# Where TensorE makes the outer products of a spline convolution that runs beside an attention: six of 32 tiles moved ahead

## The chip, the core and the metric

The kernel runs on one core of a Trainium2 chip. It is one launch. Its metric is the device time in microseconds, from start to end, of that core; a run's time is one execution, and three runs are given for the kernel before. The engines are TensorE (PE; its weight loads are PEld), VectorE (DVE), ScalarE (ACT), GpSimd (POOL) and SyncE (SP). Each runs its own stream of instructions, and they wait for one another by semaphores.

## What is computed

The reference is a graph network of four layers on 3125 nodes with 32 features and 103,125 edges: an attention, a mean aggregation in two steps, a mixture of Gaussians, and a spline convolution. The part that matters here is one stage in which two things are computed edge by edge, both sorted by target node.

```python
# attention (layer 0), per head; src is the target of the sum
e = leaky_relu(a_src[:, src] + a_dst[:, dst] + fc_b)
e = exp(e - seg_max(e, src)[:, src])
out = segment_sum(e * hp[:, dst, :], src) / segment_sum(e, src)
# second spline convolution (inside layer 3): 64 -> 64 features, K = 125 = 5**3 kernel points
basis, idx = spline_basis(pseudo)          # 8 of 125 weights per edge
msg[e] = sum_s basis[e, s] * (h[col[e]] @ W[idx[e, s]])
out = segment_sum(msg, row) / deg + b
```

The kernel writes the eight weights of an edge as a row of 125 (mostly zero). Then the sum over edges of (basis row) x (feature row) is a 125 x 64 matrix, an outer product per chunk of edges, and the weights W are applied to it afterwards.

## The kernel before, in words

The stages run one after the other. The change touches only `stage_attention_spline` (L840), which runs once, and in it only the stream of TensorE, with the helper `outer_products` of the class `Spline` (L1380), which other stages call too, without the new argument.

**Tiling.** The sorted edges lie in chunks of 16 slots of one target node. A tile is 128 slots, that is 8 chunks; a block is 32 tiles (TB), so 256 chunk columns; there are 37 blocks, two in each turn of a hardware loop, the last one behind it.

**One block n, engine by engine.**

- POOL gathers the table rows of the far ends (`gather`, L940 to L951): 32 indirect DMAs, one a tile, into one of two buffers. It may start when the sums (`summed`) and the spreads (`sl.spreads`) of the block that last used the buffer are made.
- ScalarE copies out the attention term (L1122), takes the exponentials (L1126), copies the weighted sums out of PSUM (L1135, two copies, semaphore `copied`), takes two small exponentials (L1140), copies the turned rows of block n-1 (L1114) and then the outer products, two copies for each pair of tiles, 32 in all (L1460, `outers`), and the turned spline rows (L1466).
- VectorE makes the scores (L1065 on), the basis rows in two halves (L1330), two of the eight spreads of features over chunks (`sl.spread(..., lead)`, L1351, four tiles each), then the probabilities spread over chunks (L1079, `spreads`), the running sums of block n-1 (L1036, L1361), the factors, and the six other spreads. A spread from the third on waits until the products of the four tiles that used its buffer are made.
- SP loads records, near ends and factors.
- TensorE (`one`, L981): turns the term (L989); applies the spline weights to the outer products of block n-1 (`through_weights`, L1418, 64 matmuls in the program); turns the exponentials (L994); makes the 32 weighted sums (L999); turns the rows of block n-1 (`turn_rows`, L977, and `sl.turn`, L1431); makes the outer products of block n (L1405), two a tile, 64 in all. A float32 matmul shows as two in the trace, except where its moving side is turned against the identity.

**What sets the order** is the code: each engine's stream is written out by hand, and nothing reorders it.

**PSUM.** The outer products go round three pairs of banks, two tiles a pair (0 and 1, 2 and 3, 4 and 5). Banks 4 and 5 also hold the weighted sums. So the tiles 4 and 5 wait until ScalarE has copied the sums (`third=(copied, n + 2)`), and from tile 6 on each pair waits for the copies (`outers`) of the pair before it in the same banks. The weighted sums of block n+1 need no such wait on the outer products, since `through_weights` has waited for them all.

**Names in the profile.** at_bank is any PSUM bank; at_spread and at_far are the spread probabilities and the gathered rows; p_spread, p_basis and p_outer belong to the spline.

Of the kernel before, what the change touches and what calls it, by code (L numbers as in the profile page):

```python
# [31 lines left out]
TB = 32  # L32
# [807 lines left out]
def stage_attention_spline(nc, g, weights, sums64):  # L840

    o = g.R
    C8, S, V = o.per_tile, o.chunk, o.vb
    W, parts = 4 * (F + 1), V // P
    with ExitStack() as c:
# [38 lines left out]
        turned, shifts, probs, turned_back, spreads, summed, copied = (  # L886
            sem(n) for n in ("turned", "shifts", "probs", "turned_back", "spreads", "summed", "copied"))
        rec_v = o.rec.rearrange("(p t) w -> p t w", p=P)
        sl = Spline(nc, c, g, "p_2", 64, 64, sums64, shared=(rec, far, F + 5, far_in, 16 * TB))
# [5 lines left out]
        with nc.Block() as block:  # L895
# [66 lines left out]
            def _(pe):  # L962
# [18 lines left out]
                def one(n, b, first=False):  # L981

                    pe.wait_ge(terms, n + 1)
                    pe.wait_ge(shifts, n + 1)
                    if not first:

                        pe.wait_ge(spreads, n)
                        pe.wait_ge(rows_copied, n)
                    nc.tensor.transpose(turned_square, term[:].rearrange("p t h -> p (t h)"), g.ident[:]).then_inc(turned, 1)  # L989
                    if not first:  # L990
                        sl.through_weights(pe, n - 1)

                    pe.wait_ge(probs, n + 2)
                    nc.tensor.transpose(turned_square, prob[:], g.ident[:]).then_inc(turned_back, 1)  # L994

                    pe.wait_ge(spreads, n + 1)
                    pe.wait_ge(copied, n + 1)
                    for t in range(TB):
                        last = nc.tensor.matmul(ps_sum[t // (TB // 2)][:, t % (TB // 2), :, :], far[b][:, t, 0:F + 1],  # L999
                                                spread[:, t, :, :], start=True, stop=True)  # L1000
                    last.then_inc(summed, 1)
                    if not first:
                        turn_rows(n - 1, 1 - b)
                        sl.turn(pe, n - 1)

                    sl.outer_products(pe, n, third=(copied, n + 2))

                one(0, 0, first=True)
                one(1, 1)
# [172 lines left out]
class Spline:  # L1182
# [194 lines left out]
        self.nc.tensor.matmul(self.ps_shift[:].rearrange("p t d -> p (t d)"), self.o.mask_t[:],  # L1377
                              self.shift[b][:].rearrange("c t d -> c (t d)"), start=True, stop=True).then_inc(self.shifts, 1)

    def outer_products(self, pe, m, third=None):  # L1380
        ring = len(self.ps_outer)
        for t in range(TB):
            if t % self.HT == 0:

                pe.wait_ge(self.bases, m * 2 + (t // self.HT + 1))
# [1092 lines left out]
```

## Time and profile before

| | us |
|---|---|
| median of 3 runs | 8911.31 |
| lowest and highest | 8875.33 and 8933.79 |
| the profiled execution | 8838.25 |
| its span | 8835.3 |

| engine | busy us | share |
|---|---|---|
| TensorE, matmuls | 5190.5 | 59% |
| TensorE, weight loads | 3677.3 | 42% |
| POOL | 4537.0 | 51% |
| VectorE | 4063.1 | 46% |
| ScalarE | 1650.5 | 19% |

The shares are of the whole program. The stage of the change takes 2,345 to 4,725 us of the span, some 27% of it, and has to be read by itself. In rows in order of time, the first number is the start, the second the length of a merged run of instructions, and the bracket the engine's idle time before it with what ended it; "issue" is time in which the engine waited for nothing that the profile shows, "remote" a release that it can't name.

### The profile page before, as it was taken

How to read it: one execution, taken by the hardware profiler on the slowest of the kernel's cores; microseconds unless marked ns; L12 is line 12 of the kernel's file. 1: busy time of each engine (PE TensorE's matmuls, PEld its weight loads, DVE VectorE, ACT ScalarE, POOL GpSimd, SP SyncE). 2: the span in 40 equal slices, each digit the busy share in tenths (PEclk: the TensorE clock that was granted, in tenths of full speed). 3: DMA queues.
4: the chain of work that ended last, by engine and by line, in shares of the span. 5: the costliest groups of instructions: out<-in, count | busy, mean ns of one | idle time of the engine just before them, and what ended most of it. 6: DMA issues, size and time to landing. Idle time of an engine off the chain costs nothing. (4 is left out here: it accounts for less than half of the span.)

```text
span 8835.3 us, 94325 instructions
## 1 busy us (share of the span) xinstructions
PE 5190.5 (59%) x31067; PEld 3677.3 (42%) x31067; DVE 4063.1 (46%) x8022; ACT 1650.5 (19%) x2811; POOL 4537.0 (51%) x4319
## 2 busy tenths in 40 slices
PE   4333333866366666666664546898887346445544
PEld 4333333645355555555543323444444224333333
DVE  6454444779444444444442213565555234433343
ACT  1111110148323232322321000000000112111111
POOL 3666664010355545555552243565553676777664
PEclk9999998679777777777776768899898667667676
DMA  3222210023311111111684533111111111111175
GB/s 67 65 65 61 63 60 19 21 91 157 87 38 37 37 36 37 36 38 37 35 36 111 203 110 139 29 30 29 28 29 26 18 15 17 17 15 18 15 14 14
DMA packets 388446, 441.45 MB, mean 50 GB/s; under 512 B 241139, under 2 KB 312320, under 8 KB 387981
## 3 DMA queue, kind: packets, MB, share of 16 engines
q0 software_dynamic: 137696, 130.26, 14.4%
q1 hardware_dynamic: 191113, 286.63, 10.1%
q10 hardware_dynamic: 59568, 23.69, 1.2%
q8 instruction: 38, 0.62, 0.0%
q14 instruction: 31, 0.25, 0.0%
HBM read 358.46 MB, written 82.34 MB: 50 GB/s over the span
## 5 line engine op out<-in xcount | busy, mean ns | idle before, releaser
L950 POOL DMA_INDIRECT at_far<-att_table,at_rec x1184 | 1268.2, 1071 | 1476.0 <-DVE p_spread L1351 714.8
L1507 POOL DMA_INDIRECT p_far<-table,p_rec x1184 | 1322.0, 1117 | 652.9 <-issue 357.8
L2137 PE MATMUL g_l_ps_sum<-g_l_row,g_l_of 128*128 128x400 f32 x3224 | 1192.3, 526 | 195.4 <-issue 170.2
L2067 POOL DMA_INDIRECT g_l_got<-table,g_l_index x806 | 805.7, 1000 | 551.6 <-DVE g_l_index L2075 308.3
L1405 PE MATMUL p_ps_outer<-p_spread,p_basis 128*25 128x40 f32 (+1 forms) x4736 | 834.5, 355 | 384.0 <-issue 236.3
L533 POOL DMA_INDIRECT rec_r<-so_r_rec,so_r_place x806 | 814.0, 1010 | 455.4 <-issue 232.1
L2137 PEld LDWEIGHTS g_l_ps_sum<-g_l_row,g_l_of 128*128 128x128 f32 x3224 | 638.9, 199 | 749.3 <-issue 301.8
L1405 PEld LDWEIGHTS p_ps_outer<-p_spread,p_basis 128*25 128x25 f32 (+1 forms) x4736 | 669.9, 190 | 554.1 <-issue 377.7
L488 PE MATMUL so_r_look<-so_r_table,so_r_lo_t 128*128 128x26 f32 x1612 | 425.1, 434 | 787.5 <-DVE so_r_table L432 745.9
L2079 DVE TENSOR_SCALAR g_l_row<-g_l_iota,edge_row 128x800 f32<-128x800 f32 x806 | 485.3, 676 | 575.3 <-remote 417.5
L488 PEld LDWEIGHTS so_r_look<-so_r_table,so_r_lo_t 128*128 128x128 f32 x1612 | 417.5, 356 | 796.8 <-DVE so_r_table L432 570.9
L1418 PE MATMUL at_bank<-p_outer,p_w 125*64 125x256 f32 x4736 | 647.7, 422 | 56.7 <-issue 51.2
L1405 PE MATMUL at_bank<-p_spread,p_basis 64*125 64x256 f32 x4736 | 655.1, 432 | 23.1 <-ACT p_outer L1460 12.3
L1351 DVE TENSOR_TENSOR p_spread<-p_far,mask_r 128x1024 f32<-128x1024 f32 x296 | 359.1, 1224 | 639.5 <-PE p_ps_outer L1405 318.1
L1460 ACT COPY p_outer<-at_bank 125x512 f32<-125x512 f32 x1184 | 589.7, 727 | 108.0 <-PE at_bank L1405 98.2
L1405 PEld LDWEIGHTS at_bank<-p_spread,p_basis 64*125 64x125 f32 x4736 | 540.3, 210 | 129.0 <-ACT p_outer L1460 33.3
L1418 PE MATMUL p_ps_out<-p_outer,p_w 125*32 125x256 f32 (+1 forms) x2738 | 375.7, 440 | 307.1 <-issue 235.2
L1418 PEld LDWEIGHTS at_bank<-p_outer,p_w 125*64 125x64 f32 x4736 | 438.8, 152 | 254.7 <-issue 167.7
L999 PE MATMUL at_bank<-at_spread,at_far 128*33 128x32 f32 x2368 | 200.4, 227 | 550.0 <-issue 489.6
L1460 ACT COPY p_outer<-p_ps_outer 125x512 f32<-125x512 f32 x592 | 345.6, 586 | 810.8 <-PE p_ps_outer L1405 389.7
L1351 DVE TENSOR_TENSOR p_spread<-at_far,p_mask 128x1024 f32<-128x1024 f32 x296 | 359.1, 1223 | 258.1 <-PE at_bank L1405 245.9
L999 PEld LDWEIGHTS at_bank<-at_spread,at_far 128*33 128x33 f32 x2368 | 153.8, 141 | 598.9 <-issue 535.6
(456 smaller groups left out, 5907.8 us busy)
## 6 DMA issues: line engine op xcount, KB each, us to landing
adjacent<-ad_by_chunk SPq DMA_DIRECT2D x74, 800.0 KB, 3.3
so_r_row<-pad_src SPq DMA_DIRECT2D x62, 832.0 KB
g_l_counts<-adjacent SPq DMA_DIRECT2D x60, 800.0 KB
g_l1d_counts<-adjacent SPq DMA_DIRECT2D x59, 800.0 KB
so_r_low<-pad_lo_src SPq DMA_DIRECT2D x62, 416.0 KB
at_far<-att_table,at_rec POOLq DMA_INDIRECT x1184
p_far<-table,p_rec POOLq DMA_INDIRECT x1184
rec_r<-so_r_rec,so_r_place POOLq DMA_INDIRECT x806
```

What stands on the lines that cost most here:

```text
L488: last = nc.tensor.matmul(ps_look[b][:, j, :], lo_t[b][:, :, j], table[b][:, :, j], start=True, stop=True)
L533: pool.indirect_dma_start(out=o.rec[:, :], out_offset=bass.IndirectOffsetOnAxis(ap=place[b][:, j:j + 1], axis=0), in_=rec[b][:, j, :], in_ ...
L950: pool.indirect_dma_start(out=far[b][:, t, :], out_offset=None, in_=g.att_table[:, :], in_offset=bass.IndirectOffsetOnAxis(ap=rec[b][:, t, ...
L999: last = nc.tensor.matmul(ps_sum[t // (TB // 2)][:, t % (TB // 2), :, :], far[b][:, t, 0:F + 1], spread[:, t, :, :], start=True, stop=True)
L1351: nc.vector.tensor_mul(self.spread_to[s % 2][:], rows.unsqueeze(3).to_broadcast(bx), self.mask[:].unsqueeze(1).unsqueeze(1).to_broadcast(b ...
L1405: last = self.nc.tensor.matmul(to.rearrange("k f c -> k (f c)"), basis[part, t % self.HT, :], rows[part, t % self.XT, :, :].rearrange("p f ...
L1418: last = self.nc.tensor.matmul(to, self.w[:, f, :], self.outer[:, f, :], start=(f < self.G), stop=(f >= self.J - self.G))
L1460: self.nc.scalar.copy(to[:, :, :, r, :], self.ps_outer[q % len(self.ps_outer)][r][:]).then_inc(self.outers, 1)
L1507: pool.indirect_dma_start(out=sl.far[b][:, t, :], out_offset=None, in_=table[:, :], in_offset=bass.IndirectOffsetOnAxis(ap=sl.rec[b][:, t, ...
L2067: pool.indirect_dma_start(out=got[b][:, j, :], out_offset=None, in_=table[:, :], in_offset=bass.IndirectOffsetOnAxis(ap=index[b][:, j:j + ...
L2079: last = nc.vector.tensor_scalar(row1[b][:, j, :], iota[:], g.edge_row[:, bass.ds(step * HB + j, 1)], None, ALU.is_equal)
L2137: last = nc.tensor.matmul(ps_sum[k][:], of4[b][:, j, :, :].rearrange("p k f -> p (k f)"), row1[b][:, j, k * COLS:(k + 1) * COLS], start=Fa ...
```

## The change

TensorE's order within a block is another one. The first four tiles' outer products are made after the turned exponentials and ahead of the weighted sums, tiles 4 and 5 between the sums and the turning of rows, and the other 26 after the turning. `outer_products` takes the range of tiles; its waits are the same, each in front of the same tile. The first block of all has no turning. All stages that call `outer_products` without a range are as before. The other engines' instructions and their order are unchanged.

```diff
@@ stage_attention_spline, tensor, one(n, b)
                     pe.wait_ge(probs, n + 2)
                     nc.tensor.transpose(turned_square, prob[:], g.ident[:]).then_inc(turned_back, 1)
 
+
+                    sl.outer_products(pe, n, tiles=range(0, 2 * sl.BT))
+
                     pe.wait_ge(spreads, n + 1)
                     pe.wait_ge(copied, n + 1)
                     for t in range(TB):
                         last = nc.tensor.matmul(ps_sum[t // (TB // 2)][:, t % (TB // 2), :, :], far[b][:, t, 0:F + 1],
                                                 spread[:, t, :, :], start=True, stop=True)
                     last.then_inc(summed, 1)
+
+                    sl.outer_products(pe, n, third=(copied, n + 2), tiles=range(2 * sl.BT, 3 * sl.BT))
                     if not first:
                         turn_rows(n - 1, 1 - b)
                         sl.turn(pe, n - 1)
-
-                    sl.outer_products(pe, n, third=(copied, n + 2))
+                    sl.outer_products(pe, n, tiles=range(3 * sl.BT, TB))
 
@@ class Spline
-    def outer_products(self, pe, m, third=None):
+    def outer_products(self, pe, m, third=None, tiles=range(TB)):
         ring = len(self.ps_outer)
-        for t in range(TB):
+        for t in tiles:
```

Here `sl.BT` is 2. In the program's order on TensorE, one block of the loop reads so before, from the turned exponentials (L994) to the first products that wait for the sums' copy:

```order
L994 MATMUL at_bank<-ident,at_prob 128x128 [waits at_probs]
L999 MATMUL at_bank<-at_spread,at_far 33x32 [waits at_copied,at_spreads]
L999 MATMUL at_bank<-at_spread,at_far 33x32 x31
L977 MATMUL at_bank<-ident,at_run 128x33 [waits at_scanned,at_rows_copied]
L977 MATMUL at_bank<-ident,at_run 128x33 x7
L1431 MATMUL at_bank<-p_fold,p_run 128x64 [waits p_2_scanned,p_2_copied]
L1431 MATMUL at_bank<-p_fold,p_run 128x64
L1385 ISA
L1388 ISA [waits p_2_bases]
L1405 MATMUL at_bank<-p_spread,p_basis 125x256 [waits p_2_spreads]
L1405 MATMUL at_bank<-p_spread,p_basis 125x256 x7
```

and so with the change (its lines are numbered up to 5 higher: L995 is L994 before, L1003 is L999, L1410 is L1405):

```order
L995 MATMUL at_bank<-ident,at_prob 128x128 [waits at_probs]
L1390 ISA
L1393 ISA [waits p_2_bases]
L1410 MATMUL at_bank<-p_spread,p_basis 125x256 [waits p_2_spreads]
L1410 MATMUL at_bank<-p_spread,p_basis 125x256 x7
L1003 MATMUL at_bank<-at_spread,at_far 33x32 [waits at_copied,at_spreads]
L1003 MATMUL at_bank<-at_spread,at_far 33x32 x31
L1393 REGISTER_ALU
L1410 MATMUL at_bank<-p_spread,p_basis 125x256 [waits at_copied,p_2_spreads]
L1410 MATMUL at_bank<-p_spread,p_basis 125x256 x3
```

Eight matmuls, tiles 0 to 3 (16 in the trace), now stand ahead of the 32 sums, with the waits for the bases and the first spread; the four of tiles 4 and 5, with the wait for the sums' copy, follow the sums directly.

The second place is the turning of rows and what follows it. Before, the products of tiles 4 and 5 led straight on to tile 6 with its wait for the product copies:

```order
L1388 REGISTER_ALU
L1405 MATMUL at_bank<-p_spread,p_basis 125x256 [waits at_copied,p_2_spreads]
L1405 MATMUL at_bank<-p_spread,p_basis 125x256 x3
L1403 ISA
L1405 MATMUL at_bank<-p_spread,p_basis 125x256 [waits p_2_outers]
L1403 REGISTER_ALU
L1405 MATMUL at_bank<-p_spread,p_basis 125x256 [waits p_2_outers]
```

With the change the turning (L978 and L1436, before L977 and L1431) comes between them:

```order
L978 MATMUL at_bank<-ident,at_run 128x33 [waits at_scanned,at_rows_copied]
L978 MATMUL at_bank<-ident,at_run 128x33 x7
L1436 MATMUL at_bank<-p_fold,p_run 128x64 [waits p_2_scanned,p_2_copied]
L1436 MATMUL at_bank<-p_fold,p_run 128x64
L1408 ISA
L1410 MATMUL at_bank<-p_spread,p_basis 125x256 [waits p_2_outers]
L1408 REGISTER_ALU
L1410 MATMUL at_bank<-p_spread,p_basis 125x256 [waits p_2_outers]
```

The turning is now queued behind the wait for the sums' copy, and tile 6 behind the turning.

## Rows read from the trace of the kernel before

A, B and C are three blocks of the stage: A turns its term at 3566.65 us, B at 2991.65, C at 2412.59.

**Rows 1.** groups by line, attention stage: count, busy us, mean ns, idle before.
```profile
L950 POOL DMA_INDIRECT at_far<-att_table,at_rec x1152 | 1238.0, 1075 | 1055.2 <-DVE p_spread L1351 714.8 <-issue 340.4
...
L999 PE MATMUL at_bank<-at_spread,at_far 128*33 128x32 f32 x2368 | 200.4, 227 | 550.0 <-issue 489.6 <-DVE at_spread L1079 59.3
```

**Rows 2.** waits of the same stretch: who, for whom, us in total, times, longest.
```profile
POOL at_far L950 <- DVE p_spread L1351: 714.8, 35, 22.5
```

**Rows 3.** order of time, POOL, block A: start us, us, what, idle before.
```profile
3561.31 0.94 POOL L950 DMA_INDIRECT at_far<-att_table,at_rec  x1 [17.54 <-DVE p_spread L1351]
...
3603.87 0.94 POOL L950 DMA_INDIRECT at_far<-att_table,at_rec  x1 [0.30 <-issue]
3624.97 0.94 POOL L950 DMA_INDIRECT at_far<-att_table,at_rec  x1 [20.16 <-DVE p_spread L1351]
```

**Rows 4.** order of time, TensorE, block A.
```profile
3576.16 9.40 PE L1418 MATMUL at_bank<-p_outer,p_w 125*64 125x256 f32 x80 [0.28 <-issue]
3585.48 0.33 PE L994 MATMUL at_bank<-ident,at_prob 128*128 128x128 f32 x1
3587.81 1.39 PE L999 MATMUL at_bank<-at_spread,at_far 128*33 128x32 f32 x37 [2.00 <-DVE at_spread L1079]
...
3607.70 0.33 PE L999 MATMUL at_bank<-at_spread,at_far 128*33 128x32 f32 x3 [1.14 <-issue]
3607.95 1.06 PE L977 MATMUL at_bank<-ident,at_run 33*128 33x33 f32 x8
3608.94 1.11 PE L1431 MATMUL at_bank<-p_fold,p_run 128*128 128x64 f32 x4
3609.99 16.86 PE L1405 MATMUL at_bank<-p_spread,p_basis 64*125 64x256 f32 x128
```

**Rows 5.** order of time, TensorE, block B.
```profile
3012.06 1.90 PE L999 MATMUL at_bank<-at_spread,at_far 128*33 128x32 f32 x43 [1.60 <-issue]
...
3017.35 0.29 PE L999 MATMUL at_bank<-at_spread,at_far 128*33 128x32 f32 x2 [0.29 <-issue]
```

**Rows 6.** order of time, ScalarE, block B.
```profile
3032.98 1.06 ACT L1135 COPY at_sums<-at_bank 33x512 f32<-33x512 f32 x2 [39.16 <-remote]
```

**Rows 7.** order of time, POOL, block B.
```profile
3029.38 0.94 POOL L950 DMA_INDIRECT at_far<-att_table,at_rec  x1 [0.30 <-issue]
3048.72 0.94 POOL L950 DMA_INDIRECT at_far<-att_table,at_rec  x1 [18.40 <-DVE p_spread L1351]
```

**Rows 8.** order of time, ScalarE, block A.
```profile
3608.06 1.06 ACT L1135 COPY at_sums<-at_bank 33x512 f32<-33x512 f32 x2 [39.29 <-PE at_bank L999]
...
3609.64 0.35 ACT L1114 COPY at_rows<-at_bank 128x264 f32<-128x264 f32 x1
...
3612.11 1.07 ACT L1460 COPY p_outer<-at_bank 125x512 f32<-125x512 f32 x2 [2.11 <-PE at_bank L1405]
3613.81 14.79 ACT L1460 COPY p_outer<-at_bank 125x512 f32<-125x512 f32 x30 [0.63 <-PE at_bank L1405]
```

**Rows 9.** order of time, VectorE, block A.
```profile
3586.53 1.22 DVE L1079 TENSOR_TENSOR at_spread<-at_bank,mask_r 128x1024 f32<-128x1024 f32 x1 [6.74 <-PE at_bank L994]
...
3622.96 1.23 DVE L1351 TENSOR_TENSOR p_spread<-at_far,p_mask 128x1024 f32<-128x1024 f32 x1 [0.73 <-PE at_bank L1405]
```

**Rows 10.** windows in block A: length, busy us, granted clock, DMA share, GB/s.
```profile
3572.80:3589.80 17.00, 14.16 (x144) 11.22 (x141) 10.10 (x9) 0.00 (x0) 13.56 (x11) 1.00 0.17 34
3589.80:3613.70 23.90, 10.42 (x55) 7.32 (x56) 5.24 (x12) 3.01 (x7) 11.46 (x12) 0.50 0.17 37
3613.70:3630.80 17.10, 13.20 (x115) 11.12 (x111) 7.35 (x6) 15.28 (x32) 4.61 (x5) 1.00 0.12 29
```

**Rows 11.** order of time, TensorE, block C.
```profile
2431.58 2.40 PE L999 MATMUL at_bank<-at_spread,at_far 128*33 128x32 f32 x59 [1.32 <-issue]
...
2457.07 15.26 PE L1405 MATMUL at_bank<-p_spread,p_basis 64*125 64x256 f32 x104 [11.55 <-ACT p_outer L1460]
```

**Rows 12.** order of time, POOL, block C.
```profile
2470.52 0.94 POOL L950 DMA_INDIRECT at_far<-att_table,at_rec  x1 [16.95 <-DVE p_spread L1351]
```

## The prediction

> **What bounds the kernel now.** I read the page first, then, for the attention stage alone (2,345 to 4,725 us, 37 blocks of about 64 us), the groups by line, then each engine's order of time in one block, then three blocks that go otherwise, then the clock by windows. The groups show who repeats without slack: POOL's gathers are 1152 times 1075 ns with 340 us of short gaps between them, and 714.8 us in which POOL waits for VectorE's last spread [rows 1], in 35 waits [rows 2], so 20.4 us each. 1238.0 + 340.4 + 714.8 = 2293 us of a stage of 2377. A block is therefore 43.5 us of gathers (3561.31 to 3604.81) and then some 20 us until the next gathers may start (3624.97) [rows 3]. The change can only shorten or lengthen those 20 us.
>
> What lies in them, in the block that I call A: TensorE's outer products, weighted sums and so on go on during the gathers, but not at their own pace. The 64 weighted-sum matmuls start at 3587.81; 37 are through in 1.39 us, and the other 27 take until 3608.04, with gaps of multiples of 0.7 us that the profile puts down to "issue" [rows 4], 489.6 us in the stage [rows 1]. They end 3.2 us after the last gather of the block has been issued. That this is no coincidence shows in block B: its sums are through at 3017.64 [rows 5], yet ScalarE's copy of them, which waits for nothing else that is late, starts only at 3032.98 [rows 6], 2.7 us after the last gather ended at 3030.32 [rows 7]. Towards the end of the gathers every engine's stream is held up, and it comes free about 2.7 us after them. I call this moment the release: about 3607.5 in A.
>
> After it, in A: sums copied by ScalarE 3608.06 to 3609.12, rows turned 3607.95 to 3609.01, spline rows turned to 3610.05, outer products from 3609.99 [rows 4, 8]. ScalarE's copies of the products are back to back from 3613.81, 30 in 14.79 us, 0.493 each, 0.99 for the two of a bank pair (two tiles) [rows 8]. VectorE's last spread, which needs 24 tiles of products, starts at 3622.96 [rows 9], and the gathers 2 us later [rows 3]. So from the release on the chain is: sums, turning, ScalarE's first product copy, then ScalarE's pace. TensorE's own pace is near it: 0.1175 us a matmul at full clock (80 in 9.40 [rows 4]), 0.94 for two tiles; but at half clock, until 3613.70 [rows 10], double that, 1.88.
>
> **The change part by part.** It moves instructions on TensorE only and adds no copy, transfer or semaphore. Each of the 37 blocks keeps 128 outer-product matmuls.
>
> *Four tiles ahead of the sums.* 16 matmuls (4 tiles, two halves, two passes) at 0.1175 are 1.88 us, at full clock since the window before 3589.80 has 1.00 [rows 10]. TensorE now waits 2.33 us there (3585.48 to 3587.81) for VectorE's turning of the probabilities [rows 4, 9]. Both spreads that they need are made earlier, and the banks are free. So they are hidden: 0 us. If that cover is gone (the spread came at once), they cost 1.88 us at that place, but the sums' end is set by the release.
>
> *The sums themselves.* What counts is how many of them are done at the release. If TensorE gets through a fixed number of instructions before it, 16 more stand in front and 16 sums are left over; at the pace of the 37, 0.038 us, they cost 16 x 0.038 = 0.6 us. If instead the stream goes on being filled while TensorE is busy and stops filling while it stands, all are done early, and ScalarE's copy starts 2.7 instead of 3.25 us after the last gather [rows 3, 6, 7, 8]: -0.6 us. Nothing in this trace has TensorE busy at just that place. The waits there differ from block to block, and after a short one the sums run further before they trickle: 59 after 1.32 us idle in block C [rows 11], 43 after 1.60 in B [rows 5], 37 after 2.00 in A [rows 4]; that speaks for the second. I take -0.1 us and keep -0.6 and +0.6.
>
> *Two tiles between sums and turning.* This is where the change adds a wait. The third bank pair is the one that holds the sums, so TensorE stands until both sum copies are through: 3609.12, where before it turned rows from 3607.95 on. Then 8 matmuls at half clock, 1.88 us, to 3611.1. The turning is queued behind: 1.06 us for the attention rows gives 3612.15, and ScalarE, which waits for them in front of its product copies, copies the rows at about 3612.4 instead of 3609.64, 2.7 us later [rows 4, 8]. It needs its 0.35 us and a DMA command, 0.6 us as before (3609.64 to about 3610.6). Its first product copy starts at about 3613.35 against 3612.11, with three bank pairs ready. Before, the second pair began at 3613.81, delayed by TensorE at half clock; now it begins at 3613.35 + 0.99 = 3614.34. **The product copies run 0.5 us later** from there on.
>
> *26 tiles after the turning.* Tile 6 needs the first copies of the first pair (two take 1.07 us together [rows 8], so 0.6 for one and up to 1.1 for both; I take 0.75), so about 3614.1, and 1.88 us at half clock ends at 3616.0; ScalarE wants it at 3613.35 + 3 x 0.99 = 3616.3. It holds. For the next pair ScalarE would wait 0.6 us if the clock is still at half. So what was won in front (1.88 us of work at full clock that was 3.76 at half) is used up: it had been TensorE's time, and the end was ScalarE's. I take +0.55 for the whole chain after the sums, bounds -0.1 (TensorE's own chain: turned at 3613.2, 72 matmuls, 8 of them at half clock, 1.88 + 64 x 0.1175 = 9.4, 3622.6 against 3622.7) and +1.1 (0.5 + 0.6).
>
> *VectorE* has its third spread free earlier, since four tiles are done; its later ones follow the pace above. Its spread of the probabilities, row updates and the DMA queues of SP and ScalarE keep their order; the two row stores go out some 2.7 us later and are needed a block later. The copy of the term, weights and the next turning (ScalarE's tail) move by the same 0.5 us, beside the gathers: 0.
>
> *Three blocks of 37 like B* lose what they had. There TensorE turned rows and made products before the release, and the wait for VectorE was 18.40 us [rows 7] instead of 20.4. Now the turning stands behind a copy that ScalarE makes only at the release: 3 x 2.0 = 6 us.
>
> Sum: 36 x (-0.1 + 0.55) + 6 = 22 us. The profiled execution took 8838.25 us (span 8835.3), so 8860 in its terms; it lies 73 us under the median of the three runs, 8911.3 (8875.3 to 8933.8), on which I put the forecast: **8933 us**. About 1% (89 us) is what a measurement of this kernel can tell from no change.
>
> **The rivals.**
> 1. *The sums finish early and ScalarE does not fall behind*: -0.6 and -0.1 a block, 36 x -0.7 = -25, less 6 lost: 8892 us. For: the blocks with short waits. Against: the copy of rows is moved behind 8 matmuls and 1.1 us of waiting. 0.18.
> 2. *A fixed number of instructions before the release and the full delay after it*: +0.6 + 1.1 = 1.7, x 36 + 6 = +67: 8978 us. For: the 27 sums that trickle at 0.7 us. Against: the trickle comes after standing still. 0.16.
> 3. *Clearly faster*: block C. Its ScalarE got its copies through in the midst of the gathers; TensorE stood 11.55 us for the next product copy [rows 11], and POOL waited 16.95 us [rows 12]. If filling TensorE's wait made every block so: 36 x (16.95 - 20.4) = -124: 8787 us, 1.4% faster. Against: C was the second block, and in B ScalarE got nothing though the sums were done. 0.04.
> 4. *Clearly slower, by the clock.* It is half from 3589.80 to 3613.70 and full then, 5.7 us after TensorE became busy without a pause [rows 4, 10]. The change puts two pauses there (1.1 us for the sums' copy, about 0.9 us for tile 6). If these keep the clock at half until the end of the products, the nine pairs from tile 6 to tile 23 take 1.88 us: 3614.1 + 16.9 = 3631.0, and the last spread comes 8 us later: 36 x 8 = +288: 9199 us, 3.2% slower. It decides from the point where the clock is not full by about 3616.3, where ScalarE wants tile 6's pair; each further pair at half costs 0.9 us. Against: in the window up to 3589.80 TensorE stands 2 us before the sums, and the clock is full throughout [rows 4, 10]; it falls in the trickle, not in that pause. 0.06.
>
> The Trainium skill (TensorE: Matmul & The Clock Gate, HAM oscillation — how this bites in real kernels) speaks for rival 4: waits between groups of matmuls let the clock fall, and every group starts slow. By that rule, the trace agrees that the clock falls while the sums trickle; whether pauses of 1 us keep it low, no row here shows.
>
> **How the numbers follow.** The forecast has 0.52, rivals 1 to 4 have 0.18, 0.16, 0.04 and 0.06, and 0.04 is left for a mere shift of all runs. The runs scatter by some 30 us around their median. From rival 1 less 30 to rival 2 and some 25: 8862 to 9003, which leaves out rivals 3 and 4 and some of the shift. Faster by over 1%: rival 3, 0.04. Slower by over 1%: rival 4 and a little of rival 2, 0.08. The rest, 0.88, is within.
>
> **What would show it.** 16 outer products between the turned probabilities and the sums, starting within 0.2 us of the former. TensorE idle about 1.1 us before the 8, released by ScalarE. The rows' copy about 4.3 us after the sums end (1.6 before). POOL's wait for the last spread: 20.4 us before, 20.9 expected; under 19.9 speaks for rival 1, over 21.7 for rival 2, under 18 for rival 3, over 25 for rival 4, with a granted clock at half beyond the first pair after the turning. I would be wrong altogether if ScalarE's copy of the sums began well before the last gather's end, or if the 43.5 us of gathers themselves changed.

## The result, and the profile after

| | us |
|---|---|
| the kernel before, median of 10 runs | 8885.85 (8856.58 to 8933.79) |
| the changed kernel, median of 10 runs | 8990.35 (8959.49 to 9037.11) |
| ratio, 95% interval | 1.012 (1.0097 to 1.0144) |
| profiled execution of the changed kernel | 8987.28, span 8985.1 |

The change costs 1.2%, 104 us, where 22 us were forecast and "within 1%" had 0.88. Compared twice more, on two chips, it gave 1.0113 (1.0086 to 1.014) and 1.011 (1.0078 to 1.0142), so the sign is not in doubt. 8990.35 lies within 8862 to 9003, but the change is nearly five times as large as forecast; the kernel before, measured beside it, had 8885.85, some 25 us under the median on which the forecast was put.

The groups by line of the stage, and its waits, in the changed kernel (they answer to [rows 1, 2]):

```profile
L951 POOL DMA_INDIRECT at_far<-att_table,at_rec x1168 | 1240.2, 1062 | 1215.3 <-DVE p_spread L1356 870.0 <-issue 345.3
...
L1003 PE MATMUL at_bank<-at_spread,at_far 128*33 128x32 f32 x2368 | 159.8, 238 | 605.6 <-issue 388.8 <-DVE at_spread L1084 216.6
```
```profile
POOL at_far L951 <- DVE p_spread L1356: 870.0, 35, 28.0
```

The gathers are what they were: 1062 ns each against 1075, and short gaps of 0.3 us. POOL's wait for the last spread grew from 714.8 to 870.0 us, by 155.2; the span grew by 149.8 (8985.1 - 8835.3). The loss is in the 35 waits: 24.9 us each instead of 20.4. One block of the changed kernel on TensorE and ScalarE, in order of time (the places of [rows 4, 8]):

```profile
3660.72 3.57 PE L1003 MATMUL at_bank<-at_spread,at_far 128*33 128x32 f32 x64 [17.89 <-DVE at_spread L1084]
3665.84 1.13 PE L1410 MATMUL at_bank<-p_spread,p_basis 64*125 64x256 f32 x8 [1.55 <-ACT at_sums L1140]
3666.78 0.67 PE L978 MATMUL at_bank<-ident,at_run 33*128 33x33 f32 x8
3667.38 1.11 PE L1436 MATMUL at_bank<-p_fold,p_run 128*128 128x64 f32 x4
3669.95 14.37 PE L1410 MATMUL at_bank<-p_spread,p_basis 64*125 64x256 f32 x104 [1.46 <-ACT p_outer L1465]
```
```profile
3664.64 1.06 ACT L1140 COPY at_sums<-at_bank 33x512 f32<-33x512 f32 x2 [43.63 <-DVEq L1045]
...
3668.29 0.35 ACT L1119 COPY at_rows<-at_bank 128x264 f32<-128x264 f32 x1
...
3669.31 3.03 ACT L1465 COPY p_outer<-at_bank 125x512 f32<-125x512 f32 x6 [0.67 <-ACT at_rows L1119]
3672.54 1.07 ACT L1465 COPY p_outer<-at_bank 125x512 f32<-125x512 f32 x2 [0.20 <-PE at_bank L1410]
3674.23 11.85 ACT L1465 COPY p_outer<-at_bank 125x512 f32<-125x512 f32 x24 [0.62 <-PE at_bank L1410]
```

Two waits stand where the diff put them: 1.55 us for the sums' copy ahead of the 8 matmuls of tiles 4 and 5, and 1.46 us for the first product copy ahead of tile 6. ScalarE copies three ready bank pairs back to back and then waits for TensorE twice, 0.20 and 0.62 us. This block shows one thing more: TensorE stood 17.89 us for VectorE's spread probabilities. In this execution they came over 5 us after the turned exponentials (called late from here on) in 30 of 33 blocks; in two later profiles of the same kernel in 5 of 33, with ratios nearly as high. So the terms are read from the last pair of profiles below.

### The profile page after: what moved, and what is told of

Same layout as the page of the kernel before. It is cut to its first block and busy times, and to the rows that moved or that the text cites. A ratio compares the mean times of both kernels' runs of the same rounds, so it can differ in the third digit from the quotient of the medians.

```text
span 8985.1 us, 94325 instructions
## 1 busy us (share of the span) xinstructions
PE 5210.8 (58%) x31067; PEld 3736.3 (42%) x31067; DVE 4064.9 (45%) x8022; ACT 1660.2 (18%) x2811; POOL 4548.7 (51%) x4319
## 5 line engine op out<-in xcount | busy, mean ns | idle before, releaser
L1410 PE MATMUL p_ps_outer<-p_spread,p_basis 128*25 128x40 f32 (+1 forms) x4736 | 825.7, 353 | 354.4 <-issue 204.1
L1410 PEld LDWEIGHTS p_ps_outer<-p_spread,p_basis 128*25 128x25 f32 (+1 forms) x4736 | 665.1, 188 | 520.5 <-issue 354.6
L1410 PE MATMUL at_bank<-p_spread,p_basis 64*125 64x256 f32 x4736 | 695.0, 443 | 99.8 <-ACT at_sums L1140 48.2
L1423 PE MATMUL at_bank<-p_outer,p_w 125*64 125x256 f32 x4736 | 678.6, 438 | 72.1 <-issue 67.7
L1410 PEld LDWEIGHTS at_bank<-p_spread,p_basis 64*125 64x125 f32 x4736 | 586.6, 216 | 166.5 <-issue 72.1
L1423 PEld LDWEIGHTS at_bank<-p_outer,p_w 125*64 125x64 f32 x4736 | 466.1, 158 | 274.0 <-issue 184.4
L1003 PE MATMUL at_bank<-at_spread,at_far 128*33 128x32 f32 x2368 | 159.8, 238 | 605.6 <-issue 388.8
L1003 PEld LDWEIGHTS at_bank<-at_spread,at_far 128*33 128x33 f32 x2368 | 142.7, 156 | 636.4 <-issue 410.8
```

Source lines behind the costliest of these rows:

```text
L1410: last = self.nc.tensor.matmul(to.rearrange("k f c -> k (f c)"), basis[part, t % self.HT, :], rows[part, t % self.XT, :, :].rearrange("p f ...
L1423: last = self.nc.tensor.matmul(to, self.w[:, f, :], self.outer[:, f, :], start=(f < self.G), stop=(f >= self.J - self.G))
```

## The experiments

All ratios are to the kernel before on the same chip, with 95% intervals. Means over blocks are over the 33 blocks of the loop whose gathers wait (the two first left out), worked out from the rows of each trace. "Copy" is the start of ScalarE's copy of the sums after the end of the block's last gather, in us; "the hold-up" is what the prediction describes, the slow trickle of the other engines' streams towards the end of the gathers, and "the release" its end.

**Which half of the change costs?** `e1` keeps the four tiles ahead and puts the turning right behind the sums; `e2` has nothing ahead and makes tiles 0 to 5 between sums and turning; `e3` is the changed kernel with TensorE's wait for the spread probabilities in front of the four tiles; `e4` is e1 with that wait. As edits of the changed kernel:

```diff
 e1, e4, behind the sums:
-  sl.outer_products(pe, n, third=(copied, n + 2), tiles=range(2 * sl.BT, 3 * sl.BT))
   if not first: turn_rows(n - 1, 1 - b); sl.turn(pe, n - 1)
-  sl.outer_products(pe, n, tiles=range(3 * sl.BT, TB))
+  sl.outer_products(pe, n, third=(copied, n + 2), tiles=range(2 * sl.BT, TB))
 e2:
-  sl.outer_products(pe, n, tiles=range(0, 2 * sl.BT))
-  sl.outer_products(pe, n, third=(copied, n + 2), tiles=range(2 * sl.BT, 3 * sl.BT))
+  sl.outer_products(pe, n, third=(copied, n + 2), tiles=range(0, 3 * sl.BT))
 e3, e4, ahead of the sums:
-  sl.outer_products(pe, n, tiles=range(0, 2 * sl.BT))
   pe.wait_ge(spreads, n + 1)
+  sl.outer_products(pe, n, tiles=range(0, 2 * sl.BT))
```

(These pieces of code, and those below, are cut to the lines that matter.)

> Four tiles' outer products stay ahead of the weighted sums, the other 28 go back behind the turning of rows, so that no wait stands between the sums and the turning. Theory W (waking): when TensorE goes straight on after the turned exponentials, VectorE's spread of them (median 2.1 us after in the kernel before, 14.9 in the changed one) comes late, and with it the sums. Then this kernel keeps that: median about 15 us, sums ending about 3 us later than before; but the product copies start sooner after the sums, so POOL's wait is about 22 us (20.4 before, 24.9 changed) and the time about 1.006 of before. Rival T (turning): the loss comes from the wait between sums and turning. Then this kernel is at or under before (ratio 0.995 to 1.000). Rival N (number): only the number of TensorE instructions ahead of the sums' end counts; like W here in the sums (16 more ahead).

> Nothing ahead of the sums; the tiles 0 to 5 all stand between the sums and the turning. Theory W: VectorE's spread comes 2 us after the turned exponentials as before and the sums end as before; the turning is queued behind 24 matmuls at half clock and the sums' copy (about 5.6 us), so the first product copy comes some 3.8 us later than before, of which 0.7 is won back: POOL's wait about 23.5 us, ratio about 1.012, by another way than in the changed kernel. Rival T: the same, and it would be the whole of the changed kernel's loss. What tells them apart is the median from turned exponentials to VectorE's spread: 2 (W), and whether the loss per tile of delay is as large as that of the changed kernel.

> The changed kernel with one edit: TensorE waits for VectorE's spread before the four tiles, not after them. Number and order of TensorE's instructions are the same. Theory W: VectorE is awake again (median about 2 us), 48 of 64 matmuls of the sums are through at the release, POOL's wait is 22.2 us (20.4 + 0.6 + 1.2), ratio 1.007. Rival N: the number is the same, so sums and waits are as in the changed kernel: VectorE late by 13 to 15 us, POOL's wait 24.9, ratio 1.012 or more, since the 1.9 us are no longer hidden.

> TensorE waits for VectorE's spread, makes four tiles, the sums, turns rows at once, and makes the other 28 tiles. Theory W: VectorE awake (median about 2 us), sums end 0.6 us later, product copies start 1.9 us sooner relative to the sums: POOL's wait about 19.1 us, ratio about 0.995, faster than before. Rival N: sums end 3 us later as in the changed kernel: POOL's wait 21.5 to 22, ratio 1.005.

| | ratio | copy | copy to next gathers |
|---|---|---|---|
| e1, ahead only | 0.9982 (0.9951 to 1.0013) | 5.49 | 15.77 |
| e4, wait, ahead only | 0.9968 (0.9937 to 0.9999) | 5.45 | 15.26 |
| e2, between only | 1.007 (1.0041 to 1.01) | 4.53 | 18.54 |
| e3, changed, wait first | 1.01 (1.0065 to 1.0135) | 5.50 | 18.43 |

e1 and the changed kernel differ only in where tiles 4 and 5 stand. The first is level with before, the second 1.2% slower; e4 and e3, compared on one chip, differ in the same way alone, 0.9968 against 1.01. So the loss needs tiles between the sums and the turning. e1 had been expected at 1.006 and e3 at 1.007 by the theory that VectorE's lateness carries the loss; neither came. From the sums' copy to the next gathers, the order with the turning right behind the sums takes 15.3 to 15.8 us, the order with tiles between them 18.4 to 18.6, and the kernel before 17.05, since it has no products ready. e1 shows both sides of the four tiles ahead: its copy comes later than before (5.49 us against 3.3 to 3.5 in the two profiles of before), and the ready products give about 1.3 us back.

**Does VectorE's lateness carry it, and does the hold-up?** I suspected for a while that the probabilities were late because the exponentials are turned behind all of the weights. `f1` (before) and `f2` (changed) turn them after half of the weights; `f6` adds to f1 the order of e4; `f3` is e1 with the exponentials turned behind the four tiles. In f1, f2 and f6 `through_weights` takes a range, with its waits in front of the first half.

```diff
 f1, f2, f6, the head of the block:
-  sl.through_weights(pe, n - 1)
+  sl.through_weights(pe, n - 1, range(0, 32))
   pe.wait_ge(probs, n + 2)
   nc.tensor.transpose(turned_square, prob[:], g.ident[:]).then_inc(turned_back, 1)
+  sl.through_weights(pe, n - 1, range(32, 64))
 f3, from e1:
+  sl.outer_products(pe, n, tiles=range(0, 2 * sl.BT))
   pe.wait_ge(probs, n + 2)
   nc.tensor.transpose(turned_square, prob[:], g.ident[:]).then_inc(turned_back, 1)
-  sl.outer_products(pe, n, tiles=range(0, 2 * sl.BT))
```

> The kernel before with one edit: TensorE turns the exponentials after 32 of the 64 weight matmuls, not after all. Theory L (late hold-up): in 198 blocks of six kernels VectorE's spread follows the turned exponentials by 0.4 to 3.4 us where these come 19 us or more before the end of the block's gathers, by 7 to 20 us where they come 17.5 us or less before it; so the order of the matmuls behind them is not what delays VectorE, but when they come. Here they come some 28 us before the end: VectorE spreads as soon as its own two spreads are done, the sums start right behind the weights and end well before the last gather, POOL's wait falls from 20.4 to 18.4 us or less (as in block B), ratio 0.992 or less, down to 0.986 if ScalarE too gets through. Rival: the hold-up catches the sums anyway, ratio 1.000, since ScalarE's copy of them is released only after the gathers.

> The changed kernel with the same single edit. Theory L: VectorE is no longer late, the sums are through at the release; what is left of the loss is the turning behind the sums' copy: POOL's wait about 21.2 us instead of 24.9, ratio to before about 1.003. Rival W (TensorE's matmuls right after the turned exponentials keep VectorE from waking): here weight matmuls follow them at once, so VectorE is late by 10 us or more and the ratio stays at 1.010 to 1.012.

> As the kernel with four tiles ahead and the turning directly after the sums (measured 0.998), but the turned exponentials come after those four tiles, 1.9 us later. Theory L: they now come 17 us or less before the gathers' end in both kinds of block, VectorE's spread follows by 10 us or more in both (in the kernel measured: 4 in even blocks, 13 in odd ones), sums end later, POOL's wait about 22.3 us (21.2 there), ratio about 1.003 to 1.006. Theory W: TensorE stands still after the turned exponentials as in the kernel before, so VectorE follows after 2 to 4 us, and the ratio is about 1.000 or under.

> The version that the runs so far point to: exponentials turned after half of the weights, TensorE waits for VectorE's spread (long made by then), four tiles, sums, turning at once, 28 tiles. Theory L: sums through before the release, product copies start 2.6 us after it (5.3 after the last gather, 7.2 before) with two bank pairs ready: POOL's wait 17.5 to 18 us, ratio about 0.988. Rival: what 16 more instructions ahead cost the sums in the hold-up eats it: ratio 0.995.

These four met a chip on which the kernel before takes 7487.5 us. Ratios: f1 1.0021 (1.0009 to 1.0033), f2 0.9993 (0.9984 to 1.0002), f3 1.0 (0.9991 to 1.001), f6 0.9996 (0.9987 to 1.0005). f1 had been expected at 0.992 or less. No difference of 1% between orders came, and the trace of f3 shows what is missing (the sums on TensorE, in order of time):

```profile
3357.89 0.33 PE L997 MATMUL at_bank<-ident,at_prob 128*128 128x128 f32 x1
3359.54 2.27 PE L1002 MATMUL at_bank<-at_spread,at_far 128*33 128x32 f32 x64 [1.32 <-DVE at_spread L1082]
```

and its POOL in the groups from 2,300 to 4,400 us:

```profile
L951 POOL DMA_INDIRECT at_far<-att_table,at_rec x1014 | 1169.0, 1153 | 390.3 <-issue 303.5 <-DVE p_spread L1354 86.8
```

All 64 sums run in 2.27 us without a gap: no engine is held up here, the chain of a block is nearly through when its gathers are, and POOL waits 86.8 us in nearly the whole stage where it waited 714.8 [rows 1]. The 1% does not come: f2, with the changed order, is even some 0.3% faster than f1 with the old one (7482.54 against 7507.69 us), clear of the noise, and why was not looked into. As far as these pairs go, the loss exists only with the hold-up; the changed kernel itself was not run on this chip. `g1` (before) and `g2` (changed) test that on a chip that has it, by gathering one tile a block instead of 32 from the third block on, which leaves out part of the work; waits that count the gathers are lowered to fit.

```diff
-  for t in range(TB):
+  for t in range(1 if reused else TB):
       pool.indirect_dma_start(out=far[b][:, t, :], ...
```

> The kernel before, but from the third block on POOL gathers only the first of the 32 tiles of a block; the other rows are left from the first blocks (this part of the computation is left out). Theory H (the hold-up comes from the gathers): no 'issue' gaps of 0.7 us in TensorE's sums, which are through in under 4 us; ScalarE copies them at once; a block is bound by TensorE's own chain, some 19 + 2 + 3 + 2 + 17 + 4 = 45 us instead of 64, so the program is about 36 x 19 = 700 us shorter, ratio about 0.92. If the sums still trickle, the hold-up has another source.

> The changed kernel with the same part left out. Theory H and L: without the hold-up VectorE's spread is not late, so the change has only its plain terms: TensorE's wait for VectorE is filled (gain up to 1.9 us), the turning stands behind the sums' copy and 8 matmuls (loss 1.1 to 3 us). Against the same kernel in the old order: -1 to +1 us a block, within 40 us of it. If the full 4.4 us a block (160 us) stay, the loss has nothing to do with the gathers.

Measured 0.9169 (0.9112 to 0.9225) and 0.9172 (0.9119 to 0.9226), medians 8171.0 and 8197.65 against 8925.0. One block of g1 on TensorE:

```profile
3379.18 0.33 PE L994 MATMUL at_bank<-ident,at_prob 128*128 128x128 f32 x1
3380.83 2.27 PE L999 MATMUL at_bank<-at_spread,at_far 128*33 128x32 f32 x64 [1.32 <-DVE at_spread L1079]
```

Without the stream of gathers the sums again run at their pace on a chip with the hold-up; it takes the gathers to make it. The medians of the two orders lie 27 us apart and the ratios 0.03%; with four runs of each that is no difference clear of noise, but a loss of 1% (some 90 us) would have shown.

The edits of f1, f2 and f6 were then run on a chip with the hold-up as h1, h2 and h4, the changed kernel beside them as h0.

> The changed kernel itself. Where the kernel before takes about 8.9 ms (engines held up during the gathers): 1.012 as measured. Where it takes about 7.49 ms (no hold-up): theory L gives 0.999 to 1.004, since only the turning's delay is left and much of a block is hidden beside 43.5 us of gathers; if the loss did not need the hold-up, 36 x 2.9 = 104 us would be 1.014.

> The order before, exponentials turned after 32 of the 64 weight matmuls; run for a chip with the hold-up. Theory L: VectorE's spread comes without delay, the sums are through well before the last gather, POOL's wait 18.4 us or less against 20.4, ratio 0.992 or less. Rival: ScalarE's copy of the sums is released only after the gathers, ratio 1.000. On a chip without the hold-up 1.002 was measured.

> The changed order with the same single edit, for a chip with the hold-up. Theory L: VectorE is not late, the sums are through at the release, POOL's wait about 21.2 us instead of 24.9, ratio about 1.003. Theory W: VectorE late by 10 us or more, ratio 1.010 to 1.012. On a chip without the hold-up 0.999 was measured.

> Early exponentials, wait for VectorE's spread, four tiles, sums, turning at once, 28 tiles; for a chip with the hold-up. Theory L: POOL's wait 17.5 to 18 us, ratio about 0.988. Rival: 16 more instructions ahead in the hold-up eat it, 0.995. On a chip without the hold-up 1.000 was measured.

| | ratio | copy | copy to next gathers |
|---|---|---|---|
| h0, changed | 1.0113 (1.0086 to 1.014) | 4.24 | 18.67 |
| h1, early exponentials, old order | 0.9963 (0.9936 to 0.9989) | 3.07 | 15.25 |
| h2, early exponentials, changed order | 1.0098 (1.0072 to 1.0125) | 3.98 | 18.63 |
| h4, early exponentials, wait, four tiles, turning behind the sums | 0.9961 (0.9935 to 0.9988) | 3.49 | 15.21 |

In h0 and h2 VectorE is late by over 5 us in 5 and in 0 of 33 blocks, and both are 1% slower: my theory of the lateness falls as the cause of the loss. It had put h2 at 1.003 and h1 and h4 at 0.992 and 0.988. h1 and h2 differ only in the change, 0.9963 against 1.0098. In 30 of 33 blocks of h1 all sums are through at the release and TensorE is already turning rows; ScalarE then finds products ready and runs without a pause (ScalarE, in order of time):

```profile
3640.91 1.06 ACT L1137 COPY at_sums<-at_bank 33x512 f32<-33x512 f32 x2 [39.89 <-remote]
3642.50 0.35 ACT L1116 COPY at_rows<-at_bank 128x264 f32<-128x264 f32 x1
3643.55 15.77 ACT L1464 COPY p_outer<-at_bank 125x512 f32<-125x512 f32 x32 [0.70 <-PE at_bank L1407]
```

That is what the prediction had seen in block B and called rare. In h2 the sums are as early in 13 blocks and it helps little (22.6 us of wait a block against 22.9 in h0), since the turning stands behind ScalarE's copy.

**Is it the rows' late copy, or the pauses?** In `k3` the attention rows are turned right behind the sums, then come tiles 4 and 5, then the spline rows are turned; otherwise it is h4. The kernel before, the changed one and h1's edit ran beside it as k1, k2 and k4.

```diff
 k3, from h4:
-  turn_rows(n - 1, 1 - b); sl.turn(pe, n - 1)
-  sl.outer_products(pe, n, third=(copied, n + 2), tiles=range(2 * sl.BT, TB))
+  turn_rows(n - 1, 1 - b)
+  sl.outer_products(pe, n, third=(copied, n + 2), tiles=range(2 * sl.BT, 3 * sl.BT))
+  sl.turn(pe, n - 1)
+  sl.outer_products(pe, n, tiles=range(3 * sl.BT, TB))
```

> The kernel before, unchanged, as a second profile on the chip on which the changed one is profiled too. Ratio 1.000. If the later sums belong to the change, its sums' copy starts about 3.1 to 3.5 us after the last gather as in the first profile, and POOL's wait is 20.4; if they are scatter between executions and chips, 4 to 5 us and a wait of 21 to 22 are to be seen here too. From the sums' copy to the next gathers 17.1 us either way.

> The changed kernel, unchanged. Ratio 1.012 with the hold-up, POOL's wait 2.8 us above that of the kernel before on the same chip (104 us over 36 blocks): 18.6 us from the sums' copy to the next gathers (17.1 before), so 1.6 for the turning behind the copy, and 1.2 for the sums' later end. On a chip without the hold-up (kernel before 7.49 ms): the ratio is what the order costs by itself; 0.999 to 1.004, since the kernel with early exponentials and this order had 0.999 there.

> Early exponentials, four tiles ahead of the sums, the attention rows turned right behind them, then tiles 4 and 5 with their wait, then the spline rows turned, then the rest. The wait for the sums' copy (1.1 us) now holds up only the spline rows, for which nobody waits until the block's end. Against the kernel with all rows turned at once (0.996): the same stretch from sums' copy to gathers, 15.2 us, since ScalarE's pace rules it; ratio 0.996, not better by more than 0.2%. If it is 18 us, it is the spline rows and not the attention rows whose delay costs.

> The order before with early turned exponentials (0.996 with the hold-up, 1.002 without it), again, to see whether its gain stands on another chip: 0.993 to 0.999; in most blocks all 64 sums are through before the last gather's end and POOL's wait is 18.0 to 18.8 us.

k3 had been expected to be like h4, 15.2 us from copy to gathers and 0.996. Measured: k1 0.9998 (0.9981 to 1.0016), k2 1.011 (1.0078 to 1.0142), k3 1.0005 (0.9979 to 1.003), k4 0.995 (0.993 to 0.9969). POOL's waits in the stage, k1 and then k2:

```profile
POOL at_far L950 <- DVE p_spread L1351: 703.9, 35, 21.8
```
```profile
POOL at_far L951 <- DVE p_spread L1356: 802.8, 35, 24.8
```

98.9 us more; from the first to the last turning of a term the stage takes 97.7 us more, and the ratio gives 97. (The spans of these two executions, 8842.6 and 8899.7, lie only 57.1 apart, since the stages that the change does not touch differ by 40 us the other way.) The terms, each a mean over blocks in us, the last column being the return of the granted clock to full after the start of the sums' copy:

| | copy | to the first product copy | to the ninth | to the last spread | gathers after it | clock full |
|---|---|---|---|---|---|---|
| k1, before | 3.28 | 3.80 | 4.84 | 6.26 | 2.01 | 6.2 |
| k2, changed | 4.37 | 5.22 | 4.76 | 6.59 | 2.01 | 10.5 |
| k3, split | 3.34 | 2.62 | 5.44 | 6.84 | 2.02 | 9.4 |
| h4 | 3.49 | 2.62 | 4.35 | 6.23 | 2.02 | 6.1 |

k3 starts its product copies as early as h4 and gives 1.7 us back behind them (16.9 us from copy to gathers). The one pause that it adds, 0.81 us in the mean for the sums' copy, stands where TensorE would be working off the start of the next pairs, and the clock returns 3.3 us later. One block of k3, TensorE and then ScalarE:

```profile
3680.61 2.08 PE L1412 MATMUL at_bank<-p_spread,p_basis 64*125 64x256 f32 x8 [0.25 <-ACT at_sums L1142]
```
```profile
3685.77 1.07 ACT L1469 COPY p_outer<-at_bank 125x512 f32<-125x512 f32 x2 [0.71 <-PE at_bank L1412]
```

So a late copy of the rows isn't needed for a loss. That the clock carries this part shows within the runs too: from the first product copy to the last spread k2 takes 10.6 to 10.8 us in the 15 blocks where the clock is full within 10 us of the sums' copy, and 11.8 in the 18 where it takes 11 to 12; in h4 it is 10.1 where it is full within 5 us and 11.1 where it takes 7. The block of k2 on TensorE, ScalarE, and two windows (length, busy of five engines, granted clock):

```profile
3632.93 0.33 PE L995 MATMUL at_bank<-ident,at_prob 128*128 128x128 f32 x1
3633.19 2.00 PE L1410 MATMUL at_bank<-p_spread,p_basis 64*125 64x256 f32 x16
3635.27 0.80 PE L1003 MATMUL at_bank<-at_spread,at_far 128*33 128x32 f32 x19
...
3655.17 1.28 PE L1003 MATMUL at_bank<-at_spread,at_far 128*33 128x32 f32 x19 [0.49 <-issue]
3657.69 2.08 PE L1410 MATMUL at_bank<-p_spread,p_basis 64*125 64x256 f32 x8 [1.24 <-ACT at_sums L1140]
3659.53 1.00 PE L978 MATMUL at_bank<-ident,at_run 33*128 33x33 f32 x8
3660.46 1.11 PE L1436 MATMUL at_bank<-p_fold,p_run 128*128 128x64 f32 x4
3662.33 15.11 PE L1410 MATMUL at_bank<-p_spread,p_basis 64*125 64x256 f32 x104 [0.75 <-ACT p_outer L1465]
```
```profile
3656.49 1.06 ACT L1140 COPY at_sums<-at_bank 33x512 f32<-33x512 f32 x2 [40.23 <-PE at_bank L1003]
3660.64 0.38 ACT L1119 COPY at_rows<-at_bank 128x264 f32<-128x264 f32 x1 [2.48 <-PE at_bank L978]
3661.69 3.03 ACT L1465 COPY p_outer<-at_bank 125x512 f32<-125x512 f32 x6 [0.67 <-ACT at_rows L1119]
3664.91 1.07 ACT L1465 COPY p_outer<-at_bank 125x512 f32<-125x512 f32 x2 [0.19 <-PE at_bank L1410]
3666.62 1.07 ACT L1465 COPY p_outer<-at_bank 125x512 f32<-125x512 f32 x2 [0.63 <-PE at_bank L1410]
3668.33 10.87 ACT L1465 COPY p_outer<-at_bank 125x512 f32<-125x512 f32 x22 [0.63 <-PE at_bank L1410]
```
```profile
3666.00:3668.00 2.00, 2.00 (x12) 1.83 (x10) 0.14 (x1) 1.07 (x2) 0.00 (x0) 0.50 0.00 0
3668.00:3670.00 2.00, 2.00 (x20) 1.87 (x17) 1.23 (x1) 1.67 (x4) 0.00 (x0) 0.96 0.00 0
```

And the same places of k1:

```profile
3669.34 0.72 PE L999 MATMUL at_bank<-at_spread,at_far 128*33 128x32 f32 x10 [1.20 <-issue]
3669.99 1.06 PE L977 MATMUL at_bank<-ident,at_run 33*128 33x33 f32 x8
3670.98 1.11 PE L1431 MATMUL at_bank<-p_fold,p_run 128*128 128x64 f32 x4
3672.02 16.86 PE L1405 MATMUL at_bank<-p_spread,p_basis 64*125 64x256 f32 x128
```
```profile
3670.10 1.06 ACT L1135 COPY at_sums<-at_bank 33x512 f32<-33x512 f32 x2 [39.65 <-PE at_bank L999]
3671.68 0.35 ACT L1114 COPY at_rows<-at_bank 128x264 f32<-128x264 f32 x1
3674.14 1.07 ACT L1460 COPY p_outer<-at_bank 125x512 f32<-125x512 f32 x2 [2.11 <-PE at_bank L1405]
3675.85 14.79 ACT L1460 COPY p_outer<-at_bank 125x512 f32<-125x512 f32 x30 [0.63 <-PE at_bank L1405]
```
```profile
3674.00:3676.00 2.00, 2.00 (x14) 1.61 (x12) 0.15 (x1) 1.23 (x3) 0.00 (x0) 0.54 0.11 38
3676.00:3678.00 2.00, 2.00 (x22) 1.77 (x20) 1.41 (x2) 2.00 (x5) 0.00 (x0) 1.00 0.28 97
```

k1's last stretch has 10 sums, k2's 19. In k1 TensorE works without a pause from 3669.34 and the clock is full some 6 us after the sums' copy. In k2 the two pauses (1.24 and 0.75 us) come in between, the clock is full only from 3668, 11.5 us after its copy, and pairs 3, 4 and 5 (counted from 0) come at half clock, their copies 1.71 us apart (3664.91, 3666.62, 3668.33): ScalarE waits 0.19, 0.63 and 0.63 us.

The version that beats both is the kernel before with the exponentials turned after half of the weights: 0.9963 and 0.995, on two chips; on the chip without the hold-up it is 0.2% slower (f1).

## Why the prediction was wrong, step by step

Before, the wait was 20.18 us in k1; changed, 22.95 in k2: +2.77 a block, where the sum had +0.45. Rows of k1 and k2 below are those of the table.

- **Four tiles ahead of the sums**, 0: their own place cost nothing, as said; in k2 they stand in TensorE's wait (3633.19, 2.00 us). All of their price is in the next step.
- **The sums themselves: failed.** Taken at -0.1; measured +1.09 (3.28 to 4.37). The choice was between a stream that goes on being filled and a fixed number of matmuls before the release, and I took the first on three blocks. The release is taken here as 2.6 us after the last gather's end. Where VectorE is on time (within 5 us), 61.5 of 64 sums are through at the release in k1 (60.8 in the first profile of before), 43.9 in k2, 44.7 in h0, 41.3 in e1, 42.0 in e3, and 59.3 in e2, which has nothing ahead. The 16 matmuls put in front of the changed kernel leave 16 to 18 behind, whether TensorE had been standing there or not. Each one left delays the copy by 0.055 to 0.066 us (slope over the blocks of the two profiles of before, of k2 and of h0), the pace of half clock: 19 in 1.28 us above. 17 x 0.06 = 1.0. The bound of +0.6 had been priced at the pace of the first 37, at full clock. A fixed number is no rule for every order, though: with early exponentials 62.6 are through in h1, and with the same 16 in front 59.2 in h4, 59.8 in k3 and 49.7 in h2; what decides between these was not found.
- **Two tiles between sums and turning**: held. The first product copy was to come 5.29 us after the sums' copy (3613.35 - 3608.06) and came 5.22 after; the rows' copy 4.3 and came 4.16.
- **26 tiles after the turning: failed**, the step that says of tile 6's pair "It holds". Three ready pairs were to win back 0.7 of the 1.24 us, since TensorE would have the next ones in time. Next to nothing was won back: to the ninth copy k2 takes 4.76 us against k1's 4.84, and 0.33 more behind it. The whole chain after the sums took +1.67 (1.42 - 0.08 + 0.33) where +0.55 was taken and +1.1 was the bound. The 0.6 us of waiting that stood under "if the clock is still at half" came, and more than once, since the clock came back 4.3 us later than before. e1, without the two pauses, had it back after 6.8 us and lost nothing. (The sum's 1.88 us for a pair at half clock was too dear: in its own rows the first two copies of pairs start 1.70 us apart, 3612.11 and 3613.81. That error went the other way.)
- **VectorE**: its later spreads followed ScalarE's pace, as said. **Gathers** unchanged, as said.
- **Three blocks like B**, 6 us: small and right in kind; k1 has 6 such blocks and k2 none.

Of the rivals, **rival 2** is what happened, in both of its parts: fixed number and full delay. Its +67 us was still too small for the 104 measured, since both parts came larger (+1.09 and +1.67 where it had +0.6 and +1.1); that its 8978 lies so near 8990.35 is in part the luck of the base, which was 25 us too high. It had a wait over 21.7 us (22.7 to 24.9 measured) and a chance of 0.16. Rival 1 fell with the copy at 4.37 us, rival 3 didn't come. **Rival 4** came in part: pauses of 0.75 to 1.5 us did delay the clock's return, but not to the end of the products, and its price was at most about 1.1 us a block in ScalarE's waits (4.76 against 3.96 for four pairs back to back, and 0.33 behind them), not 8; h4, without these pauses, has 0.4 of that too. The Trainium skill (TensorE: Matmul & The Clock Gate, HAM oscillation — how this bites in real kernels) has the clock fall in waits between groups of matmuls, so that the next group starts slow. In k1 and k2 the clock was at half before the pauses came; what they show is that it came back later with them (full after 6.2 and after 10.5 us). I had given this all or nothing, where it belonged into the forecast as a shift of a few microseconds.

What stays open: what holds the engines up during the gathers. g1 shows that the gathers make it, f3 that it is absent on one chip; what it consists of no run shows. Loading of code would be an obvious source, but the DMA view of k1 from 2,600 to 4,580 us lists no packet of an instruction queue, and the sums trickle there all the same. Nor is it shown why VectorE's probabilities are late in some executions.

## What to carry to other kernels

Where engines are held up to a known moment, count the instructions that stand in front of the critical ones: here each one put ahead left about one more behind that moment, even though it filled a wait, and where the held-up stream came early enough (h4, k3) most of that price was gone. And look at which wait stands in front of short work that another engine needs at once: two tiles behind the sums' copy cost 2.8 us a block after that copy, the same two behind the turning nothing. A pause of about a microsecond right after such a moment put the clock's return off by some 3 to 4 us in k3 and k2, so price the work in that stretch at half.

## What the runs showed of the hardware

- The same kernel before takes 8839.48 to 8925.0 us (medians of five comparisons, on at least three chips) and 7487.5 us on another. From the first to the last turning of a term the stage takes 2318 us in before and 1769 in f3, some 550 of the 1,360 us between these executions; the rest lies in other stages and was not looked into. In the stage the hold-up stands out: TensorE 489.6 us "issue" in front of the sums [rows 1] and none in f3, with gathers of 1075 and 1153 ns.
- The hold-up needs the gathers (g1: 64 sums in 2.27 us) and ends 2.2 to 3.6 us after the last of them in nearly all blocks of all orders (last gap among the sums, before, after, k1, k2, h0, e1, e2).
- Of a stream that is held up, 16 matmuls placed ahead displaced 16 to 18 behind them (before and k1 against k2 and h0), but only 3 where the exponentials were turned early (h1 against h4).
- While the granted clock is at half, pairs of product copies start 1.71 us apart, held by TensorE; at full clock ScalarE's own 0.99 rules (k1, k2). The sums run 19 in 1.28 us at half (k2) and 37 in 1.39 us at full [rows 4].
